# Transformer block on one core: residuals of two output projections added by TensorE through the identity

## The reference

```
x = L0(x, ctx, ctx, mask)      # 16 heads of 64, softmax over queries' keys, output projection, + x
x = L1(x, ctx)                 # gated fusion with the mean of ctx, layer norm
x = L2(x, ctx, ctx)            # 16 heads of 16, causal, relu, + x, norm with the unbiased deviation
x = L3(x, ctx):
    sa = attention(x, x, band of 64 keys, head slopes) @ swo + sbo
    x  = layernorm(x + sa) * g1 + be1
    ca = attention(x, ctx, no mask) @ cwo + cbo
    x  = layernorm(x + ca) * g2 + be2
    return layernorm(x + gelu(x @ w1 + b1) @ w2 + b2) * g3 + be3
```

## Time and profile before

| | before |
|---|---|
| median of 3 runs | 1574.02 us |
| lowest, highest | 1570.39, 1574.12 us |
| the profiled execution: its own time | 1575.49 us |
| its span, first to last instruction | 1573.7 us |
| mean granted TensorE clock | 0.978 of full speed |
| busy: TensorE, VectorE, ScalarE, GpSimd | 91%, 55%, 45%, 17% |

### The profile page before, as it was taken

One profiled execution on the slowest core, in us unless ns is written; L12 is line 12 of the kernel. 1 busy time (PEld: TensorE's weight loads), 2 busy tenths in 40 slices (PEclk: granted clock), 3 DMA queues, 4 the chain that ended last, 5 costly groups with the idle time before them and its releaser, 6 DMA issues.

```text
span 1573.7 us, 24180 instructions
## 1 busy us (share of the span) xinstructions
PE 1424.6 (91%) x8296; PEld 713.7 (45%) x8328; DVE 864.4 (55%) x2099; ACT 715.0 (45%) x1177; POOL 263.7 (17%) x138
## 2 busy tenths in 40 slices
PE   5999998888999989898999998989899999989886
PEld 2336545433533754542453464553263355455334
DVE  2662565585366266568346537557636635655761
ACT  0662263455366234427446425252825632725461
POOL 1004121301100413220110313121011030303001
PEclk9999999999999999999999999999999999999998
DMA  9000504312200230540310031242031005043210
GB/s 341 24 1 14 101 1 87 71 19 114 69 1 7 39 70 3 98 76 1 127 56 1 8 63 46 44 85 47 1 128 55 1 8 108 1 73 64 41 61 13
DMA packets 44776, 85.28 MB, mean 54 GB/s; under 512 B 10464, under 2 KB 27872, under 8 KB 44384
## 3 DMA queue, kind: packets, MB, share of 16 engines
q1 hardware_dynamic: 41136, 73.17, 18.6%
q10 hardware_dynamic: 3504, 10.39, 3.4%
HBM read 43.68 MB, written 2.10 MB: 29 GB/s over the span
## 4 chain that ended last, share of the span: by engine, by line
PE 60%; DVE 16%; issue 11%; ACT 6%; DMA 3%; SPq 2%; ACTq 1%; POOL 0%; DVEq 0%; POOLq 0%
DVE nmax L1074 7%; PE obank L1295 7%; PE ring L1275 6%; PE ring L1251 6%; PE ring L1461 6%; PE ring L1285 6%; PE ring L1350 4%; PE ring L1603 4%; PE ring L1200 3%; PE obank L1511 3%; ACT q_all L770 3%; PE ring L1452 2%; DMA q_all<-q_parts 2%; SPq L412 2%; DVE rbuf L1093 2%
## 5 line engine op out<-in xcount | busy, mean ns | idle before, releaser
L1074 DVE TENSOR_REDUCE nmax<-ring 128x2 f32<-128x1024 f32 (+1 forms) x192 | 218.0, 1175 | 41.0 <-PE ring L1461 32.1
L680 ACT ACTIVATE region_e<-region_d,nmin 128x512 f32<-128x512 f32 x256 | 182.6, 714 | 79.2 <-DVE nmin L935 78.5
L783 ACT ACTIVATE region_e<-ring 128x1024 f32<-128x1024 f32 x192 | 182.9, 992 | 49.2 <-PE ring L1461 29.9
L935 DVE CUSTOM_DVE_ANT_0 region_d<-ring,maskb 128x512 f32<-128x512 f32 x256 | 166.0, 687 | 62.6 <-issue 62.6
L770 ACT ACTIVATE q_all<-ring 2x1024 fp32r<-2x1024 bf16 x96 | 97.5, 1016 | 213.6 <-PE ring L1522 213.0
L605 POOL TENSOR_TENSOR nat_x<-nat_n,rows 128x1024 f32<-128x1024 f32 x16 | 37.6, 2352 | 606.7 <-DVE nat_n L984 459.3
L1070 DVE TENSOR_REDUCE nmax<-ring 128x4 f32<-128x512 f32 (+1 forms) x96 | 86.2, 911 | 80.8 <-PE ring L1452 80.1
L1285 PE MATMUL ring<-region_q 64*128 64x512 f32 x512 | 121.2, 607 | 5.6 <-ACT region_q L667 3.3
L1452 PE MATMUL ring<-cbf 64*128 64x128 bf16 (+2 forms) x1280 | 123.2, 270 | 0.0
L1295 PE MATMUL obank<-region_e,vs 128*64 128x512 f32 x512 | 117.8, 599 | 0.0
L779 ACT ACTIVATE region_e<-ring 128x768 f32<-128x768 f32 (+1 forms) x96 | 74.0, 775 | 47.7 <-PE ring L1452 47.1
(11 more groups left out here) (193 smaller groups left out, 2154.0 us busy)
## 6 DMA issues: line engine op xcount, KB each, us to landing
q_all<-q_parts SPq DMA_DIRECT2D x192, 64.0 KB, 2.5
region_e<-in_w_f SPq DMA_DIRECT2D x8, 1024.0 KB, 5.8
k_tiles_a<-k_parts SPq DMA_DIRECT2D x96, 64.0 KB, 2.3
k_tiles_b<-k_parts SPq DMA_DIRECT2D x96, 64.0 KB, 2.3
q_all<-q_parts ACTq DMA_DIRECT2D x96, 64.0 KB, 3.2
wvo<-in_wv SPq DMA_DIRECT2D x5, 1024.0 KB, 5.0
wqk<-in_wq SPq DMA_DIRECT2D x4, 1024.0 KB, 9.2
wqk<-in_wk SPq DMA_DIRECT2D x4, 1024.0 KB, 11.0
```

What stands on the lines that cost most here:

```text
L680: ins = act.activation(e0[:, n % E0, h, :], sm0[:, n % 2, h, :], ACT.Exp, bias=nmin0[:, n, h:h + 1], scale=-1.0, accum_out=sum0[:, n, h:h ...
L783: act.activation(e16[:, n % 4, 2 * u:2 * u + 2, 0:nq], slot((a, "B", g, kt, u))[:, :, 0:nq], ACT.Exp)\
L935: ins = dve.tensor_tensor_reduce(out=sm0[:, n % 2, h, :], in0=slot(("S0", p, kt))[:, h, :], in1=maskb[:, :], scale=-1.0, scalar=3.0e38, op ...
L1074: dve.tensor_reduce(nmax[:, qt, 2 * u:2 * u + 2], slot(name)[:, :, 0:nk], AX.X, ALU.max, negate=True)\
```

## The change

For BANDED and FULL, `out_heads` waits for the residual right after it has its two slots, and four matmuls with the identity as the stationary operand write `nat_x` to PSUM; the two packs of heads are then accumulated on top. `out_heads` of CAUSAL is as before. VectorE no longer adds and copies: `bn_stats` reads each half of the projection in PSUM as soon as it is full, and the normalization reads PSUM too. The slots stay taken for longer: that of half 0 is released by a small memset after the normalization of row tile 1, that of half 1 by one after row tile 3. VectorE's own waits for `resid_ready` ahead of BANDED's and FULL's drain go away. The feed-forward's drain is unchanged.

```diff
+        done = sb("done", [1, 2])
...
-                def moments(j):
+                def moments(j, rows_of=lambda t: nat_y[:, t, :]):
 
                     for t in (2 * j, 2 * j + 1):
-                        ins = dve.bn_stats(stats[:, t, :], nat_y[:, t, :])
+                        ins = dve.bn_stats(stats[:, t, :], rows_of(t))
...
-                def norm(n):
+                def norm(n, name=None):
...
                     for t in range(NT):
-                        ins = dve.tensor_scalar(nat_n[:, t, :], nat_y[:, t, :], mv[:, t, 0:1], scale[:, t:t + 1],
+                        rows_of = slot((name, t // 2))[:, t % 2, 0:D] if name else nat_y[:, t, :]
+                        ins = dve.tensor_scalar(nat_n[:, t, :], rows_of, mv[:, t, 0:1], scale[:, t:t + 1],
                                                 ALU.subtract, ALU.mult)
                         if t + 1 < NT:
                             ins.then_inc(tile_normed, 1)
+                        if name and t == 1:
+                            dve.memset(done[0:1, 0:1], 0.0).then_inc(*ends_drain((name, 0)))
                     ins.then_inc(norm_ready, 1)
+                    if name:
+                        dve.memset(done[0:1, 1:2], 0.0).then_inc(*ends_drain((name, 1)))
...
+                def moments_out(name):
+
+                    for j in range(2):
+                        dve.wait_ge(*filled_by((name, j), b))
+                        moments(j, lambda t: slot((name, t // 2))[:, t % 2, 0:D])
+
                 attention(BANDED)
-                dve.wait_ge(resid_ready, b * 5 + 2)
-                drain_out("OS", nat_x)
-                norm(2)
+                moments_out("OS")
+                norm(2, "OS")
...
                 attention(FULL)
-                dve.wait_ge(resid_ready, b * 5 + 3)
-                drain_out("OC", nat_x)
-                norm(3)
+                moments_out("OC")
+                norm(3, "OC")
...
                     dst = [start((name, j)) for j in range(2)]
+                    if a != CAUSAL:
+                        pe.wait_ge(resid_ready, b * 5 + a + 1)
+                        for m in range(NT):
+                            pe.matmul(dst[m // 2][:, m % 2, 0:D], ident[:, :], nat_x[:, m, :], start=True, stop=False)
                     for t in range(PACKS):
...
-                                                start=(t == 0), stop=(t == PACKS - 1))
+                                                start=(t == 0 and a == CAUSAL), stop=(t == PACKS - 1))
```

## The result

| | before | changed |
|---|---|---|
| median | 1573.96 us (5 runs) | 1581.91 us (5 runs) |
| lowest, highest | 1570.39, 1574.12 | 1580.6, 1587.15 |
| the profiled execution: its own time | 1575.49 | 1580.6 |
| its span | 1573.7 | 1578.7 |
| mean granted TensorE clock | 0.978 | 0.982 |

The changed kernel is slower: ratio 1.0062, 95% interval 1.0043 to 1.008, or +7.95 us between the medians against the +6.7 us forecast. Runs of one kernel spread by several us (6.6 here, 3.7 before), so the places of the change are read first, from the timeline, and the total afterwards.

A forecast was written before the change was run, and what follows sets the result against it. TensorE was taken to set the end, VectorE's drains being covered: +1.04 - 0.20 = +0.84 us at each of eight places, +6.7 us, giving 1580.7 us after allowing for the profiled run's offset from the median; range 1577 to 1586.

The forecast's parts named there:

- The identity records: Ends of BANDED and FULL: four fp32 matmuls, eight TensorE records of 0.216 us, delay V0 by 1.04 us a place.
- The transposes: Behind the fillers: eight transposes run in a row, no longer in step with VectorE's norms, -0.20 us a place.
- VectorE's drains: Two drains of 0.69 us a place go; worth nothing by themselves, as the V0 tile covers them.
- The gate: Before fillers and transposes: X needs half 0's slot, released after row tile 1's norm; open by 0.14 us, nothing added.
- the rival that the gate shuts: PSUM reads 0.13 us slower each free half 0's slot 0.3 us late: +9.8 us, 1583.8 us; chance 0.10.
- The gap rival: Four identity matmuls under 0.68 us together fit TensorE's wait before pack two: not slower, 1572.4 us; chance 0.06.
- The total and the clock: Total +6.7 us, 1580.7 us; clock rival: low-clock spells lost or added move it to 1578.2 or 1583.2 us, chance 0.14.

The follow-up runs named there:

- the two kernels with constants: Changed kernel whose normalization from PSUM takes constant 0 for the mean, or constants for both mean and deviation; one run each: 1586.3 and 1583.07 us.
- the late release: Changed kernel with the slot of half 0 released only after the fourth row tile is normalized, with that of half 1: 1591.44 us, ratio 1.0104.

## Why the prediction was right, point by point

**The identity records: right.** 24 records in a row, V0 at 5.28 us: the sum had 5.28, the shift +1.04. All eight places show it. With the records out it goes, with the records alone it is there, twice the records cost 1.73 us more.

**The transposes: right**, 1.04 us instead of 1.24, -0.20 a place. So +0.84 a place is what the timeline shows (11.05 - 10.21), and +6.7 us is what the places give.

**VectorE's drains: right that they were worth nothing by themselves.** The norms of the changed kernel start 7.27 us behind its first record, against 684.03 - 676.57 = 7.46 before.

**The gate: right in its cost, wrong in its margin.** I had it open by 0.14 us, with 15 ns for each read from PSUM; it is 0.05 us shut. Two terms were mis-sized. From the start of the norms to the memset (685.63 to 686.56) are 0.93 us, where I had 0.33 + 0.42 and 0.06 for all four reads: the moments cost 10 ns more and the norms 130. The norm's price was taken from a row (L1127) with one constant and one operation, 425 ns; with two scalars from SBUF it is 539. And from the end of the memset (686.62) to the weight load that it lets go (686.70) pass 0.08 us, which I had at nothing. All this cost nothing: the transposes start at 9.15 also in the two kernels with constants, where the wait is gone. So the rival that the gate shuts is refuted for this kernel, although its 0.13 us a read was what the norms cost more; the moments cost 0.01 (and its 8 x 1.2 is 9.6, not 9.8). Delaying the release further showed the gate real.

The VectorE page of the Trainium skill (section on the TRN2 errata) has a fixed 62 cycles more for a PSUM source, an estimated 65 ns at its 0.96 GHz. The measured differences agree with it in neither case: 9 ns for the moments (423 against 414) and 131 for the norm with two scalars from SBUF. By the same page's two elements a cycle for an fp32 tensor-scalar from SBUF (section on mode 2x_2P) such a norm would take an estimated 0.2 us (58 + 128 cycles); it took 408 ns.

**The gap rival: wrong here, right as a mechanism.** Its point was 0.17 us a matmul. In fp32 one took 0.43; in fp32r 0.58/4 = 0.145, and the loss vanished. So the gap is real and the number format decides whether the work fits in. The 262 cycles that the Trainium skill gives ("TensorE: Matmul & The Clock Gate", section on the back-to-back issue gap) make an estimated 0.109 us at 2.4 GHz, near what an fp32r matmul shows here (0.145, or 0.12 without the 0.1 of the first of a row), and a quarter of an fp32 matmul's 0.43.

**The total and the clock.** The medians give +7.95 and, repeated, +7.6 against +6.7. At equal clock it is +8.1, so 1.4 us aren't found at the places. The first median is 1.2 us above the 1580.7 of the forecast; that it is so near is in part luck, since single runs of the changed kernel lie between 1577.68 and 1587.36. What the clock does is visible in the stage from BANDED's projection to FULL's: in the repeated changed kernel it took 83.13 us in the second sequence and 85.80 in the third, with the same instructions and a clock of 0.98 and 0.94 (third last column):

```profile
1060.62:1146.42 85.80, 74.09 (x384) 28.98 (x382) 53.97 (x77) 42.83 (x46) 5.56 (x3) 0.94 0.15 27
677.98:761.11 83.13, 71.41 (x384) 28.42 (x382) 53.93 (x77) 42.83 (x46) 5.57 (x3) 0.98 0.16 29
```

I had priced such spells only in the stretch ahead of BANDED's projection (1.25 us each) and left FULL's out, where the slower of these two has three such spells against one and 2.7 us more. This was the thin part of the forecast. A mean clock also doesn't say what a spell costs. The same stretch of the kernel before, then twice of the changed kernel, all with a clock of 0.96:

```profile
294.22:376.96 82.74, 71.05 (x376) 27.29 (x374) 54.61 (x77) 42.80 (x46) 5.55 (x3) 0.96 0.15 28
294.54:378.13 83.59, 72.15 (x383) 28.95 (x381) 53.96 (x77) 42.83 (x46) 5.57 (x3) 0.96 0.16 29
678.36:762.72 84.36, 72.67 (x384) 28.71 (x382) 53.90 (x77) 42.83 (x46) 5.56 (x3) 0.96 0.16 28
```

In the first two the low clock falls in one piece (0.50 from 329.2 to 336.0 and from 330.5 to 337.3), and the difference is 0.85 us, one place's shift. In the third it falls in two pieces, the second of them later in the stretch (0.51 from 716.2 to 719.6 and from 726.5 to 730.0, 0.99 between them), and the stretch is 0.77 us longer at the same mean. Two more sequences of this execution are like the third (84.16 and 84.18 us), so where the low clock falls makes some 1.9 us in it. Whether it also makes the 1.4 us of all runs, or something else between the places does, stays open; the other kernels deviate from their places by up to 1.3 us too, the late release by 2.0.

## What to carry to other kernels

Before work is moved from an engine that is covered to the one that sets the end, measure the room in front of the first thing that waits there: here 0.68 us, against 1.73 us of fp32 identity matmuls. In this kernel matmuls with the identity were cheap only in the form that takes one record each; in that form they fit in the gap, the lighter VectorE work starts to count, and fillers that were free become the next wait. A slot that is held over a longer chain is a gate even when it costs nothing: price the reads that stand ahead of its release with the operands they will really have.

## What the runs showed of the hardware that I had not expected

- A VectorE tensor-scalar of 128x256 from PSUM takes 418 ns with two constants, 478 with one scalar from SBUF, 539 with two; from SBUF with two scalars it takes 408.
- Four fp32r matmuls of 128x256 with the identity took 0.58 us to the start of the next group, four in fp32 1.83 us.
- After an idle wait, the first transpose started 0.44 us behind the weight load of two fillers; in a busy row 0.80 us behind it (687.50 - 686.70). So a weight load 0.91 us late moved the transposes by 0.54, and one 0.05 us late did not move them.
- The mean granted clock of single runs of one kernel went from 0.974 to 0.984, and over all nine kernels the times followed it by 1.1 us for each 0.001.
